# A decoder on one Trainium2 core: routed experts with stationary weights, and a top-64 search split in two halves

## The reference, cut to what matters

```python
g = jax.nn.softmax(h @ Wr, axis=-1)
top2_w, top2_idx = jax.lax.top_k(g, 2)
hid = jax.nn.relu(jnp.einsum('bsh,ehf->bsef', h, W1))      # 256 -> 1024
expert_out = jnp.einsum('bsef,efh->bseh', hid, W2)         # 1024 -> 256
```

```python
dots = jnp.einsum('bhij,hk->bkij', dots, pre_proj)         # 16 heads mixed
dots = jnp.where(causal[None, None], neg, dots)            # 16 memory keys + tokens
vk = lax.top_k(dots, 64)[0][..., -1:]
dots = jnp.where(dots < vk, neg, dots)
attn = jnp.einsum('bhij,hk->bkij', jax.nn.softmax(dots, -1), post_proj)
```

## Time and profile before

| | us |
|---|---|
| median of 3 runs | 3644.81 |
| lowest, highest | 3632.73, 3649.38 |
| the profiled execution, time | 3649.2 |
| the profiled execution, span of its instructions | 3647.4 |
| PE busy | 2816.1 |
| DVE busy | 2401.5 |
| ACT busy | 1113.6 |
| POOL busy | 978.2 |

### The profile page before, as it was taken

The page is one execution under the profiler, slowest core; times in us unless marked ns, Lnnn a source line. Parts: engine busy times, 40 slices in busy tenths (PEclk is TensorE's granted clock), DMA queues, the critical chain, the costliest instruction groups (busy, mean ns, idle before and its releaser), DMA issues. The chain is left out here.

```text
span 3647.4 us, 41333 instructions
## 1 busy us (share of the span) xinstructions
PE 2816.1 (77%) x12008; PEld 1875.4 (51%) x12008; DVE 2401.5 (66%) x7594; ACT 1113.6 (31%) x2881; POOL 978.2 (27%) x1242
## 2 busy tenths in 40 slices
PE   4754997299977767875787577755469989999999
PEld 2322564176764345644554455444346656666666
DVE  4995564455340999899989998999856525212112
ACT  1111563044313333433343334332232123222121
POOL 2551000300030445444544454545412210000000
PEclk7555997599976778687868787866679999999999
DMA  2000000455533211221122112111020041212212
GB/s 92 0 0 16 6 1 20 171 159 169 163 110 102 85 56 53 75 71 59 54 75 70 60 54 73 60 60 36 5 79 1 1 99 59 74 52 70 71 52 68
DMA packets 180764, 235.39 MB, mean 65 GB/s; under 512 B 35761, under 2 KB 138869, under 8 KB 180286
## 3 DMA queue, kind: packets, MB, share of 16 engines
q1 hardware_dynamic: 177470, 224.37, 19.1%
q0 software_dynamic: 3072, 8.39, 0.7%
HBM read 170.57 MB, written 62.13 MB: 64 GB/s over the span
## 5 line engine op out<-in xcount | busy, mean ns | idle before, releaser
L2063 DVE MATCH_REPLACE8 a_rest<-a_best,a_rest 128x416 f32<-128x416 f32 (+54 forms) x1308 | 603.0, 468 | 0.0
L2071 DVE MAX8 a_best<-a_rest 128x8 f32<-128x416 f32 (+54 forms) x1308 | 564.3, 472 | 0.0
L1746 PE MATMUL a_pat<-a_kp,a_probs 128*128 128x128 f32 x1344 | 292.9, 392 | 205.5 <-POOL a_kp L1965 200.3
L1746 PEld LDWEIGHTS a_pat<-a_kp,a_probs 128*128 128x128 f32 x1344 | 260.5, 289 | 286.6 <-POOL a_kp L1965 263.4
L2004 POOL TENSOR_SCALAR a_probs<-a_mixed,a_best 128x120 f32<-128x120 f32 (+12 forms) x208 | 285.7, 1373 | 334.7 <-DVE a_best L2075 304.1
L1727 PE MATMUL a_psc<-a_kT,branch 64*128 64x264 f32 (+3 forms) x640 | 226.5, 613 | 165.9 <-ACT a_stage L1829 165.2
L3131 DVE TENSOR_TENSOR tl_hT<-tl_act_out,tl_gate 128x512 f32<-128x512 f32 x128 | 88.6, 692 | 385.8 <-ACT tl_act_out L2999 385.7
L1727 PEld LDWEIGHTS a_psc<-a_kT,branch 64*128 64x128 f32 x640 | 119.3, 263 | 255.0 <-ACT a_stage L1829 230.1
L1737 PE MATMUL a_pmix<-a_rows,a_kpre 128*128 128x264 f32 (+41 forms) x528 | 181.5, 472 | 84.3 <-ACT a_mixed L1862 79.8
L2913 PE MATMUL tl_py<-tl_w,tl_hT 128*128 128x256 f32 x1024 | 241.6, 379 | 0.0
L2894 PE MATMUL tl_ph<-xT,tl_w 128*128 128x512 f32 x512 | 240.7, 592 | 0.0
(11 more groups left out here) (418 smaller groups left out, 5295.9 us busy)
## 6 DMA issues: line engine op xcount, KB each, us to landing
f_w<-in_L_ffn_W SPq DMA_DIRECT2D x39, 1024.0 KB, 5.6
tl_gate<-l_gates SPq DMA_DIRECT2D x256, 128.0 KB, 2.9
l_scores<-a_stage SPq DMA_DIRECT2D x32, 528.0 KB, 2.7
l_scores<-a_stage SPq DMA_DIRECT2D x32, 400.0 KB, 2.4
l_scores<-a_stage SPq DMA_DIRECT2D x32, 272.0 KB, 2.1
f0o_w<-in_L_ffn_W SPq DMA_DIRECT2D x8, 1024.0 KB, 12.6
sorted_x<-z_blank SPq DMA_DIRECT2D x1, 4992.0 KB, 15.6
f_xs<-sorted_x SPq DMA_DIRECT2D x39, 128.0 KB, 5.2
```

The source lines that it names most:

```text
L1746: ins = pe.matmul(pat[:, at + c, :], probs[:, g % 4, c * P:(c + 1) * P], kp[:, g % 4, :], start=True, stop=True)
L2063: last[a] = signal(dve.match_replace(rest[:, a, 0:wd], best[:, a, q - 1, :], rows_of[a] if q == 1 else rest[:, a, 0:wd], GONE))
L2071: last[a] = signal(dve.max(best[:, a, q, :], rest[:, a, 0:wd]))
```

## The change

**Experts.** DVE copies the place's first weights into a fixed buffer (`first`, two halves of 128 x 1024), in `bring(j)`, once PE has finished with the half before (`h_full`). PE takes 128 x 128 blocks of them as the stationary operand and lets the 128 rows pass by, so that the hidden features come out already transposed. The transposes L1347, the copies L1415 and PE's load of the expert's number go away; the relu writes straight to `hT`. PE's order is now `hidden(j+1)`, `turn_rows(j+2)`, `out(j)`. On ACT the row copies stand ahead of `result`, and the exponential and the sine of the tables come a round later and ahead of `result`; DVE's pieces come a round later too. The combination stage is as it was.

**Search.** For pairs whose first tile has `wd` of 344 or more (`HALVED`), `search_halves` first splits the row: elementwise maximum of its left and its right half into the first half of `rest`, elementwise minimum into the second. It takes the 64 largest of the maxima (8 MAX8, 7 MATCH_REPLACE8 on wd/2 keys) and the 32 largest of the minima (4 and 3), and gets the 64th largest of all from 33 pairwise minima and their largest (L2068, L2072 in the changed file). That holds for 12 of a sequence's 32 pairs: all 8 of i=3 and the last 4 of i=2.

```diff
 # l0_experts, PE
                 def hidden(j):
-                    e = pe.value_load(R.expert[0:1, j:j + 1], min_val=0, max_val=E0 - 1)
                     pe.wait_ge(x_ready, j + 1)
                     for half in range(2):
                         if j >= 1:
                             pe.wait_ge(h_done, 2 * (j - 1) + half + 1)
-                        for k in range(KD):
-                            w = R.w1[:, bass.ds(e, 1), k, half * 512:half * 512 + 512].rearrange("p a f -> p (a f)")
-                            ins = pe.matmul(ph[half][:], xsT[:, j % 2, k, :], w, start=(k == 0), stop=(k == KD - 1))
+                        pe.wait_ge(w1_brought, 2 * j + half + 1)
+                        for f in range(HF):
+                            for k in range(KD):
+                                ins = pe.matmul(ph[half][:, f * P:(f + 1) * P], first[half][:, k, f * P:(f + 1) * P], xsT[:, j % 2, k, :],
+                                                start=(k == 0), stop=(k == KD - 1))
                         ins.then_inc(h_full, 1)
...
                 for j in range(SLOTS):
-                    turn_hidden(j)
                     if j + 1 < SLOTS:
                         hidden(j + 1)
-                    out(j)
                     if j + 2 < SLOTS:
                         turn_rows(j + 2)
+                    out(j)
 # l0_experts, ACT
                     if j + 1 < SLOTS:
                         relu(j + 1)
-                    result(j)
                     if j + 2 < SLOTS:
                         rows(j + 2)
                     c, k = j // K.PIECES, j % K.PIECES
-                    if c < CHUNKS and k == 1:
+                    if c < CHUNKS and k == 2:
                         K.growth(act, c)
-                    if c < CHUNKS and k == 2:
+                    if c < CHUNKS and k == 3:
                         K.waves(act, c)
+                    result(j)
 # l0_experts, DVE
+                def bring(j):
+                    e = dve.value_load(R.expert[0:1, j:j + 1], min_val=0, max_val=E0 - 1)
+                    for half in range(2):
+                        if j >= 1:
+                            dve.wait_ge(h_full, 2 * (j - 1) + half + 1)
+                        w = R.w1[:, bass.ds(e, 1), :, half * 512:half * 512 + 512].rearrange("p a k f -> p (a k) f")
+                        dve.tensor_copy(first[half], w).then_inc(w1_brought, 1)
+
+                dve.wait_ge(R.w1_loaded, 16 * E0)
+                bring(0)
                 for j in range(SLOTS):
-                    if j >= 2:
-                        dve.wait_ge(y_full, j - 1)
-                    for half in range(2):
-                        dve.wait_ge(h_turned, 2 * j + half + 1)
-                        dve.tensor_copy(hT[j % 2][:, half * HF:half * HF + HF, :], pT[half][:]).then_inc(hT_ready, 1)
-                    if j // K.PIECES < CHUNKS:
-                        K.piece(dve, j // K.PIECES, j % K.PIECES)
+                    if j + 1 < SLOTS:
+                        bring(j + 1)
+                    if 0 <= (j - 1) // K.PIECES < CHUNKS:
+                        K.piece(dve, (j - 1) // K.PIECES, (j - 1) % K.PIECES)
 # l1_attention, DVE
+                def search_halves(pair, lanes):
+                    last = {}
+                    if searches(2 * pair):
+                        dve.wait_ge(found, searches(2 * pair))
+                    for a, g, wd in lanes:
+                        dve.wait_ge(cut_done, g + 1)
+                        if g >= 2:
+                            dve.wait_ge(neg_ready, g - 1)
+                        h = wd // 2
+                        x, y = mixed[:, g % DEEP, 0:h], mixed[:, g % DEEP, h:wd]
+                        last[a, 0] = signal(dve.tensor_tensor(rest[:, a, 0:h], x, y, ALU.max))
+                        last[a, 1] = signal(dve.tensor_tensor(rest[:, a, h:wd], x, y, ALU.min))
+                    for q in range(LAST + 1):
+                        for a, g, wd in lanes:
+                            h = wd // 2
+                            for part in range(2 if 2 * q <= LAST else 1):
+                                values = rest[:, a, part * h:part * h + h]
+                                if q:
+                                    top = best[:, a, q - 1, :] if part == 0 else low[:, a, 8 * q - 7:8 * q + 1]
+                                    after(last[a, part])
+                                    last[a, part] = signal(dve.match_replace(values, top, values, GONE))
+                        for a, g, wd in lanes:
+                            h = wd // 2
+                            for part in range(2 if 2 * q <= LAST else 1):
+                                values = rest[:, a, part * h:part * h + h]
+                                after(last[a, part])
+                                if q == LAST and searches(g - 1):
+                                    dve.wait_ge(masked, searches(g - 1))
+                                ins = dve.max(best[:, a, q, :] if part == 0 else low[:, a, 8 * q + 1:8 * q + 9], values)
+                                last[a, part] = signal(ins)
+                        if q == 0:
+                            after(last[lanes[-1][0], 1])
+                            dve.sem_inc(top_ready, 2)
+                        if q == TOP1 // 16 and pair >= 2:
+                            invert(pair - 2)
+                    for a, g, wd in lanes:
+                        top = best[:, a].rearrange("p q e -> p (q e)")
+                        after(last[a, 0])
+                        last[a, 0] = signal(dve.tensor_tensor(both[:, a], top[:, TOP1 // 2 - 1:TOP1][:, ::-1], low[:, a],
+                                                              ALU.min))
+                    for a, g, wd in lanes:
+                        after(last[a, 0])
+                        dve.tensor_reduce(best[:, a, LAST, 7:8], both[:, a], AX.X, ALU.max).then_inc(found, 1)
```

More of the change, by code:

```diff
@@ L1271, in l0_experts @@
         flat = G.xT[:].rearrange("p k n -> p (k n)")
-        h = [flat[:, i * F0:(i + 1) * F0] for i in range(2)]
-        hT = [flat[:, (2 + i) * F0:(3 + i) * F0].rearrange("p (f q) -> p f q", f=FT) for i in range(2)]
+        hT = [flat[:, i * F0:(i + 1) * F0] for i in range(2)]
+        first = [flat[:, (2 + i) * F0:(3 + i) * F0].rearrange("p (k f) -> p k f", k=KD) for i in range(2)]
         px = ps("px", [P, KD, P])
         ph = [ps(f"ph{i}", [P, 512]) for i in range(2)]
-        pT = [ps(f"pT{i}", [P, HF, P]) for i in range(2)]
         py = [ps(f"py{i}", [P, D]) for i in range(2)]
@@ L1334, in hidden @@
                             pe.wait_ge(h_done, 2 * (j - 1) + half + 1)
-                        for k in range(KD):
-                            w = R.w1[:, bass.ds(e, 1), k, half * 512:half * 512 + 512].rearrange("p a f -> p (a f)")
-                            ins = pe.matmul(ph[half][:], xsT[:, j % 2, k, :], w, start=(k == 0), stop=(k == KD - 1))
-                        ins.then_inc(h_full, 1)
-                def turn_hidden(j):
-                    for half in range(2):
-                        pe.wait_ge(h_done, 2 * j + half + 1)
-                        if j >= 1:
-                            pe.wait_ge(hT_ready, 2 * (j - 1) + half + 1)
-                        for f in range(HF):
-                            at = (half * HF + f) * P
-                            ins = pe.transpose(pT[half][:, f, :], h[j % 2][:, at:at + P], G.ident[:])
-                        ins.then_inc(h_turned, 1)
+                        pe.wait_ge(w1_brought, 2 * j + half + 1)
[3 more added lines that the diff above has]
+                                                start=(k == 0), stop=(k == KD - 1))
+                        ins.then_inc(h_full, 1)
                 def out(j):
@@ L1381, in relu @@
                     if j >= 2:
-                        act.wait_ge(h_turned, 2 * (j - 1))
+                        act.wait_ge(y_full, j - 1)
                     for half in range(2):
                         act.wait_ge(h_full, 2 * j + half + 1)
-                        act.activation(h[j % 2][:, half * 512:half * 512 + 512], ph[half][:], ACT.Relu).then_inc(h_done, 1)
+                        act.activation(hT[j % 2][:, half * 512:half * 512 + 512], ph[half][:], ACT.Relu).then_inc(h_done, 1)
                 def result(j):
@@ L1530, in l1_attention @@
         least = sb("least", [P, 2])
+        low = sb("low", [P, 2, 1 + TOP1 // 2])
+        both = sb("both", [P, 2, 1 + TOP1 // 2])
         probs = sb("probs", [P, 4, CH1 * P])
@@ L1582, in turned_over, with halved @@
             return TOP1 < l1_tile(g)[3] <= TOP1 + 6 * R8
+        def halved(g):
+            return l1_tile(g)[3] >= HALVED
         def searches(g):
@@ L2034, in invert @@
                     dve.reciprocal(rden[:, x], den[:, x]).then_inc(inverted, 1)
+                after(signal(dve.memset(low[:, :, 0:1], -GONE)))
                 for pair in range(PAIRS1):
@@ L2038, in _ @@
                     last = [0, 0]
+                    if halved(2 * pair):
```

(2 more changed lines are left out.)

9 lines of the change are left out of this document (4 added, 5 removed).

## The result

| | before | after |
|---|---|---|
| median, us | 3641.02 | 3605.00 |
| lowest, highest | 3629.46, 3649.38 | 3599.96, 3607.83 |
| the profiled execution, time | 3649.2 | 3601.0 |

The ratio is 0.9902, 95% interval 0.9877 to 0.9928, from 5 runs of each. A second set of runs of the same kernel gave 3598.13 and 0.9889 (0.9866 to 0.9911). The forecast was 3598.

What follows compares the result with a forecast made beforehand. PE was taken to bound the experts and DVE the attention; 3649.2 - 29 (experts) - 26 (search) + 8 (POOL handover) = 3602 for the profiled execution, which stands 4.4 above the median, so 3598 us, range 3580 to 3618.

Steps and rivals of the forecast that it cites:

- Experts, PE: Experts' rounds on PE: transposes go, narrow products at 0.112 us each, round 7.98 to 7.25 us, -29 us in all.
- Experts, the cover: Experts' weight copies on DVE stay hidden behind PE's work, about 1 us to spare in the worst round; no cost.
- the bare work: Search on DVE: a halved pair of 504/512 keys takes 17.4 us before DVE's waits for itself.
- the waits: Search: DVE's waits for itself at the start, before `top_ready` and in the final reduction, about 0.3 us a pair.
- The term for the search: Attention, halved pairs of i=3 and i=2: 6.6 us a sequence gained, -26 us for four.
- the handover: Start of halved pairs: DVE's four splits precede POOL's comparison, except in 8 pairs where DVE waits about 1 us; +8 us.
- Rival (a): Halved pairs: POOL gets in between DVE's splits, 4.6 us a pair, 221 us for the 8, result 3811; chance 0.16.
- (b): Halved pairs: POOL is first by a hair, each of 48 loses one comparison, 1.7 us; +82, result 3672; chance 0.11.
- (c): Attention: another engine, PE or the chain over POOL and ACT, takes the search's gain; result 3624; chance 0.08.
- (d): Experts: the gain doesn't come, because narrow products or late copies hold PE; result 3627; chance 0.09.

Runs made afterwards that it cites:

- `copies_twice`: Changed kernel with each of DVE's copies of the experts' weights done twice, first into a spare buffer: 3612.50 us, ratio 0.9922 to the kernel before.
- `rows_behind`: Changed kernel with the rows of place j+2 turned behind `out(j)` again, on PE and ACT: 3635.48 us, ratio 0.9979 to the kernel before.
- `splits_unbroken`: Changed kernel with DVE's waits for both tiles set ahead of the first split: 3640.93 us on the slower chip, ratio 0.9885 to the kernel before.
- `apart_top_i3`: Changed kernel, second tile's splits behind the first tile's first two MAX8, `top_ready` sent in the second round, `HALVED` 408: 3579.55 us, ratio 0.9841 to before.
- `gap_after_each`: Changed kernel with each tile's split into minima waiting for the end of its split into maxima: 3620.65 us, ratio 0.9946 to the kernel before.
- `search_alone`: Changed kernel with the experts' stage of before, the search in halves kept: 3680.53 us on the slower chip, ratio 0.9984 to the kernel before.

## Why the prediction held, by its steps

**Experts, PE: right.** The pitch was 0.112, the round 7.24. The sum said -29; behind the first second product the traces show -29.05 (274.9 for 304.0), and 2.9 more ahead of it, where the term had nothing. PE never waits for the copies: right. The expected cost and gain thus came as worked out, from the nearest row with the same operation and size.

**Experts, the cover: right in sign, its size off.** I gave the copies about 1 us to spare. The first copy ends 0.36 us ahead of the first weight load that reads it in 7 of the 8 rounds behind a piece 3, and 0.12 in the eighth. Of that 0.12 pass even where PE waits for the copy (`copies_twice`), so 0.24 and nothing are left. (The text on record for `copies_twice` says 8 rounds and one more.) The copy was faster than assumed (0.69, not 0.75), but it starts 0.78 us after the last instruction of the piece ahead of it, where the sum left some 0.3:

```profile
770.08 0.69 DVE L1059 TENSOR_TENSOR branch<-sk_angle 128x512 f32<-128x512 f32 x1
771.54 1.30 DVE L1403 COPY xT<-f0o_w 128x1024 f32 x2 [0.78 <-DVE branch L1059]
```

What the prediction passed over is that the new order on PE is needed: its sum gives the turned rows 0.22 us and no wait, wherever they stand, and `rows_behind` prices their old place at 31 us.

**Search: the bare work was right, the waits were mis-sized.** The term for the search was -26 us. With both waits out of the way, the groups of i=3 lose 6.6 us and those of i=2 0.7, 7.3 a sequence or 29 in all, and the pair takes 17.60. In the changed kernel itself -4.5 came. Two waits took the rest, `top_ready` and the handover. For `top_ready` I allowed some 0.12 us, as for any step that waits for the one before; the pair lost 0.22, and 12 us in all went there.

**The handover: the step that failed.** The prediction had DVE first by 0.04 us; it is, by 0.03. It had the four splits back to back and POOL waiting 1.3 us. In fact POOL gets in behind the second, its first comparison is longer by 0.35 (344 keys) to 0.52 us (504 keys), and DVE's third waits 0.28 to 0.41. And in the 8 pairs whose forerunner is not halved, DVE was to wait 1 us and waited 0.10 to 0.14. In the four of i=3 POOL compares only 136 keys there, which makes 0.11 us at 0.81 ns a key; in the four of i=2 it compares 328 keys but starts 0.25 us ahead of the first split. The lengthened splits add up to 12 us in 44 pairs, so +8 should have stood at 12, spread the other way round. Rival (a) named the right mechanism, POOL between the splits, and the wrong price, 4.6 us a pair: it held a comparison to shut DVE out for its whole length, as the earlier trace rows suggested. By the Trainium skill ("SBUF — State Buffer", Who interferes with whom, and Summary: rules for kernel authors) the two exclude each other until the first has finished; here the measurement differs, 0.4 of 2 us.

(b) did not come: behind a halved pair POOL was never first in the changed kernel's two traces, and where it was, in those 8 pairs, it cost 0.10 to 0.14 us. It was first once in each of three other traces (`splits_unbroken`, `apart_top_i3`, `copies_twice`), 0.21 us ahead, and the first split lost 0.21 to 0.28 us there, not 1.7. (c), another engine taking the search's gain, did not either: with DVE's waits gone the stage followed DVE. One small piece of it shows: behind each i=3 group DVE waits 0.25 us for ACT (L1870), and the pair, which is not halved, takes 8.01 us for 7.67, some 1.4 us in all. (d), no gain from the experts, did not come.

In sum the attention brought 4.5 us where 18 were forecast. In the profiled executions 3 us more from the experts and 12 from code that the change leaves alone stand against that, so they lie 48.2 us apart where 47 were forecast; the medians lie 36 and 42 apart. The fit of the number is thus in part luck: the experts carried it, and the search brought a quarter of what was forecast for it.

## What to carry to other kernels

Before counting an elementwise instruction with two inputs on DVE as its own length, look at who starts on POOL at the same moment. Here one-input work (two MAX8) put between the splits took the wait away, with the same work done. A notice that had to wait for an instruction's end cost DVE 0.22 us each time when it was sent at once, and nothing that the trace shows when it was sent a few instructions later. When products lose the work that stood between a copy and its reader, the copy has to move ahead too, or the gain goes into that wait.

## What the runs showed of the hardware

POOL's tensor-scalar comparison shuts out DVE's two-input instructions for 0.81 ns a key, 0.28 us at 344 keys to 0.41 at 504, though it lasts 1.4 to 2.0 us. In the earlier trace rows, with an elementwise POOL instruction of two inputs, DVE waited to its end. Which property makes the difference wasn't tried.

A split that followed its forerunner on DVE without a wait, up to 0.33 us behind POOL's start, went ahead of POOL; one behind a semaphore wait did not (0.77 us for 0.42 at the second split of `gap_after_each`). That DVE had already taken up the former is the reading that fits, not something that a trace shows directly.

In the four kernels that ran on the slower chip the 512 small products of the combination stage took 66 us; in all nine traces from elsewhere they took 27. The rows are of `search_alone` and of the changed kernel (busy, mean ns | idle before, releaser):

```profile
L2662 PE MATMUL sp_pk<-branch,sk_V 128*32 128x16 f32 x512 | 31.2, 211 | 37.7 <-issue 35.0 <-PEq L1284 2.7
```

```profile
L2656 PE MATMUL sp_pk<-branch,sk_V 128*32 128x16 f32 x512 | 27.5, 214 | 2.7 <-PEq L1283 2.7
```

The products are as fast; PE had nothing to issue for 35 us more. With 39 us that is most of the 45 us between the times of the kernel before on the two chips, though that kernel has no trace from the slower one. What kept the instructions back stays open: the traces name nothing, and it wasn't tried.
